# Middle attention: the probabilities are turned by plain fp32 matrix products with the identity in place of TensorE's transpose mode

## What is computed

```
q, k, v = x @ wq, x @ wk, x @ wv              # 625 x 512, 8 heads of 64
scores  = q @ k.T / sqrt(64)                  # per head, 625 x 625
attn    = softmax(scores)
out     = attn @ v
x       = x + out @ wo
```

## Time and profile before

| what | value |
|---|---|
| median of three runs | 2634.62 us |
| the three runs | 2627.95, 2638.78, 2634.62 us |
| the profiled execution, own time | 2621.18 us |
| its span, first to last instruction | 2619.2 us |
| mean granted clock of TensorE | 0.950 |
| instructions | 34595 |
| PE busy | 2457.5 us (94%) |
| DVE, POOL, ACT busy | 1802.2, 1649.6, 924.4 us |

### The profile page before, as it was taken

How to read it: one execution, slowest core, us unless ns; L and a number is a source line. 1 busy time by engine, 2 the same in 40 slices (tenths; PEclk the granted TensorE clock), 3 DMA queues, 4 the chain that set the end, 5 groups by cost and what they waited for, 6 DMA issues and landing times.

```text
span 2619.2 us, 34595 instructions
## 1 busy us (share of the span) xinstructions
PE 2457.5 (94%) x11680; PEld 2056.2 (79%) x11680; DVE 1802.2 (69%) x2675; ACT 924.4 (35%) x1128; POOL 1649.6 (63%) x724
## 2 busy tenths in 40 slices
PE   6989978976899679999999999999999999999999
PEld 6878877865799667777777777777777777777777
DVE  8974324547588657777777777777777777777775
ACT  3732224522389552223223232223222322322231
POOL 0024322228888745777777777777777777777773
PEclk9989877988799779999999999999999999999999
DMA  3024010011433200221212212122122221221211
GB/s 77 16 68 162 17 65 17 1 49 47 110 87 92 79 38 33 97 84 76 96 64 96 95 65 96 69 91 96 64 96 80 80 96 64 96 91 69 96 64 36
DMA packets 49889, 190.90 MB, mean 73 GB/s; under 512 B 13300, under 2 KB 17911, under 8 KB 33444
## 3 DMA queue, kind: packets, MB, share of 16 engines
q1 hardware_dynamic: 35728, 177.90, 19.4%
q0 software_dynamic: 13200, 10.75, 1.9%
q10 hardware_dynamic: 900, 1.44, 0.2%
HBM read 177.54 MB, written 12.35 MB: 72 GB/s over the span
## 4 chain that ended last, share of the span: by engine, by line
PE 79%; DVE 10%; POOL 6%; issue 2%; ACT 2%; DMA 1%; SPq 0%; DVEq 0%; ACTq 0%; POOLq 0%
PE PS L1698 25%; PE PS L1700 25%; PE PS L1699 25%; POOL gatW L751 3%; POOL XN L751 2%; PE PS L1776 2%; DVE hotS L1151 1%; POOL gat L751 1%; DVE hotD L1152 1%; DVE negmax L1388 1%; DVE PTl L1405 1%; PE PS L1962 1%; PE PS L1920 0%; PE PS L1963 0%; DVE XN L1115 0%
## 5 line engine op out<-in xcount | busy, mean ns | idle before, releaser
L1648 DVE SCALAR_TENSOR_TENSOR XN<-PS,attn,XN 125x512 f32<-125x512 f32 x1083 | 805.4, 749 | 439.9 <-PE PS L1700 431.4
L789 POOL TENSOR_TENSOR OPl<-TS,OPh 128x1024 fp32r<-128x1024 f32 x256 | 677.5, 2647 | 116.7 <-ACT OPh L1061 116.7
L789 POOL TENSOR_TENSOR OPl<-RAW,OPh 128x1024 fp32r<-128x1024 f32 x192 | 555.2, 2892 | 273.4 <-ACT OPh L1061 273.4
L1698 PE MATMUL PS<-OPh,XTh 128*125 128x512 f32 x1280 | 507.6, 397 | 2.0 <-DVE attn L1602 2.0
L1700 PE MATMUL PS<-OPh,XTl 128*125 128x512 f32 x1280 | 506.1, 395 | 0.0
L1699 PE MATMUL PS<-OPl,XTh 128*125 128x512 f32 x1280 | 503.7, 394 | 0.0
L1061 ACT ACTIVATE OPh<-TS 128x1024 fp32r<-128x1024 f32 x256 | 271.8, 1062 | 530.0 <-PE PS L1700 517.3
L1061 ACT ACTIVATE OPh<-RAW 128x1024 fp32r<-128x1024 f32 x192 | 203.8, 1062 | 579.1 <-PE PS L1700 579.1
L1698 PE MATMUL PS<-OPh,Sh 128*125 128x512 f32 x1024 | 404.3, 395 | 3.1 <-DVE XN L1645 3.1
L1700 PE MATMUL PS<-OPh,Sl 128*125 128x512 f32 x1024 | 403.4, 394 | 0.0
L1699 PE MATMUL PS<-OPl,Sh 128*125 128x512 f32 x1024 | 402.1, 393 | 0.0
(11 more groups left out here) (345 smaller groups left out, 3587.6 us busy)
## 6 DMA issues: line engine op xcount, KB each, us to landing
RAW<-in_values SPq DMA_DIRECT2D x64, 2048.0 KB, 7.5
filters<-filt SPq DMA_DIRECT2D x14, 672.0 KB
fil<-filters SPq DMA_DIRECT2D x11, 840.0 KB
Wraw<-in_ffn SPq DMA_DIRECT2D x4, 1024.0 KB, 5.3
Wraw<-in_L_q SPq DMA_DIRECT2D x2, 1024.0 KB, 5.1
Wraw<-in_L_k SPq DMA_DIRECT2D x2, 1024.0 KB, 8.7
Wraw<-in_L_v SPq DMA_DIRECT2D x2, 1024.0 KB, 7.3
gatW<-nodes,dstI POOLq DMA_INDIRECT x90
```

Source lines behind the costliest of these rows:

```text
L789: g.tensor_tensor(OPl[:, j], operand_source(j, parity), OPh[:, j].bitcast(F32), ALU.subtract).then_inc(op_lower, 1)
L1648: v.scalar_tensor_tensor(out=XN[:, t], in0=PS[0:P, bank, :], scalar=w, in1=XN[:, t], op0=ALU.mult, op1=ALU.add).then_inc(v_added, 1)
L1698: mm(dst, lh, rh, start=start, stop=False, skip_group_check=resumed)
```

## The change

Each of the five transposes of an item becomes an ordinary fp32 matrix product of the same two operands into the same place. The product starts and ends its own sum.

```
-                        ins = nc.tensor.transpose(dst, prob[:, turned % 4, tile_columns(t)], ident[0:P, 0:P])
+                        ins = mm(dst, prob[:, turned % 4, tile_columns(t)], ident[0:P, 0:P], start=True, stop=True)
```

## The result

Eight runs of each kernel on the same chip gave medians of 2649.4 us after and 2632.06 us before: **ratio 1.0059, 95% interval 1.0042 to 1.0077**, slower by 15.5 us (11 to 20); the two medians as they stand are 17.3 us apart. A later set, in which the changed kernel ran eight times against 23 runs of the kernel before, gave 1.0041 (1.0021 to 1.0061), 10.8 us. The forecast was 2655.8 us, +0.8% or 21.2 us: the direction and the range held, the size was too large by a third against the first set and nearly double that of the second.

What follows compares the result with a forecast made beforehand. TensorE and DVE were taken as balanced in the middle attention, so added TensorE time counts nearly at once. Terms 5.3 + 13.45 + 2.5 = 21.2 us gave 2655.8 us (+0.8%), likeliest range 2645 to 2666, outer 2636 to 2668.

Steps and rivals of the forecast that it cites:

- Two passes a block: Attention's turning: each plain fp32 product makes two passes for a transpose's one, 0.109 us each at 2.4 GHz.
- the rival of four passes: Each plain product takes four passes in place of two: 70 us added, 2705 us; chance 0.03.
- Five items at 1.2 GHz: Five items before the first head's product, at half clock with no wait to hide in: 25 x 0.21 = 5.3 us.
- Six heads: Six heads at full clock, 25 transposes each: 150 x 0.109 = 16.35 us, less 2.9 of waits, leaves 13.45.
- The wait for `prob`: TensorE's wait ahead of a head's third group of transposes, 0.56 us in one head; six total 2.9, all vanish.
- the fourth rival: Wait ahead of each head's product also shrinks, up to 5.1 us relieved: 2651 us, inside the likeliest range; no separate chance.
- The tail: Last 15 transposes, no scores between the last three groups: 1.1 + 0 + 0.34 + 1.05 us, sum 2.5.
- The clock: Whether scores and plain passes lift TensorE from 1.2 to 2.4 GHz; no lift was taken as likelier.
- The low stretch: Half-clock stretch, 417.18 to 444.48 us, said to begin after a 3.98 us standstill; expected again, with items of 4.25 us.
- rival A: Plain passes keep the clock up in the attention, saving 18.6 of 21.2 us: 2637 us; chance 0.23, whole or half.
- the dips: Half-clock falls at heads' products: phase worth 5 us below in the range; above, three more at 1.5 us each.
- the idle time ahead of A: TensorE's wait before a head's thirty products, for the last `PTl`: 0.76 us in one head, expected to stay near that.

Runs made afterwards that it cites:

- these five alone: Changed kernel's plain products for the first five items only, transposes for the other 35, against the kernel before: ratio 1.0021.
- second pair of profiles: Both kernels profiled again unchanged: kernel before at ratio 1.0017 against runs of itself, attention 138.9 us; changed kernel's attention 154.8 us.
- three blocks in five: Kernel before with only blocks 0, 1 and 4 of the five transposed, the other two left unturned: ratio 1.0051.

## Why the prediction was right, and where it was off

1. *Two passes a block, at a transpose's pace.* Right: 400 records; 0.109 us each by a head of the kernel that issues each plain product twice; the rival of four passes is out.
2. *Five items at 1.2 GHz, 5.3 us.* Right to the tenth: 23.34 - 18.08 = 5.26, in the changed kernel and with these five alone.
3. *Six heads, 13.45 us.* Right for heads without dips: the kernel before takes 14.61 to 14.76, the changed one 16.9, so 6 x 2.2 = 13.3. The wait for `prob` went as said. The wait ahead of the head's product gave no relief, against the fourth rival.
4. *The tail, 2.5 us.* The passes there cost 0.95 us (from 538.41 to 547.25 before, 561.50 to 571.29 after). The first two groups cost 1.1, as summed. The fourth and fifth, which the sum had at 0.34 and 1.05, cost nothing: the last one's five passes had run at 1.2 GHz and its ten now ran at 2.4 (2.42 us from 567.03 for both groups, for 2.47 from 542.93 with the 0.21 us wait between). That part of the miss is the clock's as well.
5. *The clock.* **This is the term that was mis-sized.** The sum took every stretch at 1.2 GHz over from the kernel before. The low stretch itself stayed ("I take no lift as likelier"), and rival A with its early rise did not come. That it began after the standstill was a wrong reading, as shown above; no term of the sum hung on it. But the dips, which I had named only as a matter of 5 us in the range, mostly went: three of 1.5 us and a last product of 5.66 for 4.29 us, and 1.0 us of the first head's product. 5.3 + 13.3 + 0.95 - 1.0 - 4.6 - 1.4 = 12.5 us, the attention's difference. In the second pair of profiles one dip and the slow end were back, and the difference was 15.9. The whole kernel's 15.5 us in the first set and 10.8 in the second are about that much, by intervals of 5 us either way. Where the dips fall was not predicted and is not explained, so that a range with room for them held is in part luck.

Rival A was half right for a reason that I had wrong: it priced three dips and the tail, which did vanish, but put it to the plain passes' kind, which the kernel with doubled transposes excludes. Of the small signs, ten passes took 1.35 and 2.46 us where 1.25 and 2.2 were named, and the idle time ahead of A was 1.17 us and not near 0.76. The expectation for three blocks in five was wrong in sign, by the same blind spot: I treated TensorE's passes as cost only.

## What to carry to other kernels

Before replacing a transpose by an fp32 product with the identity, count the passes: two for one, at the same pace, and they count in full where TensorE has no wait behind them. Where an engine's clock depends on its work, price a change in passes at both levels, and look for what ends and begins a low stretch: here the fall came ahead of a 4 us standstill or in its first 0.6 us, products in that standstill that nobody reads cut the low stretch short and took 8 us off the attention, and taking needed passes away made the kernel slower. Check in the windows when the clock fell before you name what made it fall.

## What the runs showed of the hardware that was not expected

- A transpose and a plain fp32 pass of 125 by 125 are the same to TensorE's time (0.109 us at 2.4 GHz) and to its clock (low stretches of 30.7 us with either).
- With a mix of 64-row scores and turned blocks, three passes a group let the clock fall to 1.2 GHz in every head, five held it between the heads' products, ten did not lift it, twenty did (in one profile).
- The long low stretch begins at the end of 2.9 us of 64-row scores (0.2 us before to 0.6 us after, in eleven profiles), and not after the 4 us of standstill that follow. With 28 dense products of 128 rows in that standstill it lasted 0, 3.4 and 6.8 us in three profiles, for 27.3 and 30.7.
- Dips at the heads' products came in 12 of 24 heads of 14.7 us and in 2 of 30 of those of 16.9 us, and in none of 6 of 14.6 us with the wait ahead of them filled; why is open.
